# Attention scores and outputs in 64x32 tiles of TensorE, with f16 score operands and outputs in two banks by key half

## The reference

```
q, k, v = x_norm @ wq + bq, ctx @ wk + bk, ctx @ wv + bv      # 16 heads of 16
score = einsum('bhqd,bhkd->bhqk', q, k) / sqrt(16) + mask
out   = einsum('bhqk,bhkd->bhqd', softmax(score), v)
x = x + (out @ wo + bo)                                       # layer 0, layer 1 alike
x = x + shared_experts(xn) + top2_of_8_routed_experts(xn)     # layer 0
x = x + sqrt((xn @ cos(theta + tn))**2 + (xn @ sin(phi + pn))**2)   # layer 1
```

## Time and profile before

| | us |
|---|---|
| median of 3 runs | 1350.27 (1349.95 to 1350.47) |
| profiled execution | 1350.14, its span 1348.3 |
| TensorE busy | 1285.6 (95%), 9750 matmul records |
| ScalarE busy | 1036.6 (77%) |
| VectorE busy | 737.6 (55%) |
| exponentials L829 | 770.4, x832, 1.069 each |
| outputs L1560 | 448.6, x3328, 0.611 each |
| scores L1546 | 338.3, x1664, 0.470 each, idle before them 19.0 |

### The profile page before, as it was taken

One profiled execution on the slowest core, in us unless ns is written; L12 is line 12 of the kernel. 1 busy time (PEld: TensorE's weight loads), 2 busy tenths in 40 slices (PEclk: granted clock), 3 DMA queues, 4 the chain that ended last, 5 costly groups with the idle time before them and its releaser, 6 DMA issues. The chain is left out here.

```text
span 1348.3 us, 27233 instructions
## 1 busy us (share of the span) xinstructions
PE 1285.6 (95%) x9750; PEld 611.0 (45%) x9750; DVE 737.6 (55%) x1622; ACT 1036.6 (77%) x1482; POOL 178.4 (13%) x220
## 2 busy tenths in 40 slices
PE   8999999999999999998999999879989999999995
PEld 5422332332333466767999998522223323323322
DVE  5246577577466676446666666633424644443346
ACT  3689999999999754452666666348899999999993
POOL 4111120020020111331000010523300000000000
PEclk9999999999999999999999999868989999999997
DMA  7566744534537060313343452652210110010001
GB/s 222 131 209 219 232 127 152 181 95 155 178 103 265 32 204 17 110 48 102 98 128 114 116 146 79 140 154 70 82 33 1 44 40 1 32 51 1 1 1 62
DMA packets 105889, 140.78 MB, mean 104 GB/s; under 512 B 24916, under 2 KB 77523, under 8 KB 105791
## 3 DMA queue, kind: packets, MB, share of 16 engines
q1 hardware_dynamic: 88368, 102.13, 24.9%
q0 software_dynamic: 9888, 29.76, 7.0%
q10 hardware_dynamic: 7534, 7.57, 2.0%
HBM read 77.11 MB, written 51.69 MB: 96 GB/s over the span
## 5 line engine op out<-in xcount | busy, mean ns | idle before, releaser
L829 ACT ACTIVATE prob<-banks 128x1024 f32<-128x1024 f32 (+1 forms) x832 | 770.4, 1069 | 55.6 <-PE banks L1546 37.8
L1560 PE MATMUL banks<-prob,v 128*32 128x512 f32 (+1 forms) x3328 | 448.6, 611 | 1.1 <-ACT prob L829 1.1
L1546 PE MATMUL banks<-zone,kst 52*128 52x512 f32 (+1 forms) x1664 | 338.3, 470 | 19.0 <-ACT prob L829 17.3
L1546 PEld LDWEIGHTS banks<-zone,kst 52*128 52x128 f32 (+1 forms) x1664 | 138.6, 182 | 363.0 <-ACT prob L829 324.8
L2160 PE MATMUL banks<-xsT_d,w 128*128 128x128 f16 x1776 | 124.7, 220 | 3.2 <-issue 2.9
L1560 PEld LDWEIGHTS banks<-prob,v 128*32 128x32 f32 (+1 forms) x3328 | 65.7, 108 | 130.9 <-issue 108.0
L2160 PEld LDWEIGHTS banks<-xsT_d,w 128*128 128x128 f16 x1776 | 109.6, 98 | 12.6 <-issue 8.9
L2171 PE MATMUL banks<-w,hh 128*128 128x256 f16 x592 | 107.5, 274 | 0.0
L1070 DVE RECIPROCAL late<-late 128x512 f32<-128x512 f32 x31 | 103.9, 3353 | 1.1
L1967 DVE TENSOR_TENSOR hl<-hid,hh 128x128 f16<-128x128 f32 x296 | 83.3, 291 | 32.6 <-ACT hh L1898 24.9
L1065 DVE COPY late<-banks 128x512 f32<-128x512 f32 x31 | 21.4, 690 | 143.9 <-PE banks L1560 124.5
(11 more groups left out here) (270 smaller groups left out, 1281.1 us busy)
## 6 DMA issues: line engine op xcount, KB each, us to landing
weight_parts<-late SPq DMA_DIRECT2D x54, 256.0 KB, 3.3
w<-weight_parts POOLq DMA_DIRECT2D x24, 512.0 KB, 3.8
zone<-q_parts SPq DMA_DIRECT2D x180, 64.0 KB
late<-in_L_ffn_W_r SPq DMA_DIRECT2D x43, 256.0 KB, 4.0
kst<-kparts SPq DMA_DIRECT2D x88, 100.1 KB
q_parts<-qparts SPq DMA_DIRECT2D x16, 512.0 KB, 3.8
weight_parts<-more SPq DMA_DIRECT2D x26, 256.0 KB, 3.2
slot_rows<-late POOLq DMA_DIRECT2D x14, 384.0 KB, 4.2
```

Of the source, the lines that this page charges most:

```text
L829: nc.scalar.activation(prob[0:m, t % P_RING, 2 * (n % 2):2 * (n % 2) + 2, :], score[G % S_RING][0:m, :, :], ACT.Exp, scale=0.25 / WSCALE). ...
L1546: last = nc.tensor.matmul(score[G % S_RING][0:m, a, :], kst[stack, 2 * q + n % 2, t * P:t * P + m].bitcast(F32R), qst[stack, u % Q_RING, n ...
L1560: last = nc.tensor.matmul(outp[u % 2][GROUP * j:GROUP * (j + 1), :], v[0:m, t, u % NQ, j, :], prob[0:m, (u * KT + t) % P_RING, j, :], star ...
```

## The change

**Scores.** The operands in `kst`, `qst` and their DRAM copies are f16. A group is eight matmuls (L1570): 64x32 tiles, four slices of 32 keys by two heads, all with 512 queries. **Outputs** (L1585): eight 64x32 tiles, four heads by two halves of 64 keys; each half of the keys has its own bank, so an output takes two banks. `finish` copies the first (L1082) and adds the second (L1084). The last tile's unused rows of v and its ones are filled. **PSUM**: `S_RING` = 2 groups (four banks) and two outputs of two banks. **Order**: for each t now scores 2t+2, outputs t-1, scores 2t+3, then at most one side piece. **Side pieces** are spread (`SIDE_AT`, `OUT_AT`), the out-projection is cut into four calls instead of two for each i, and a piece waits for all pieces but the one before it. The scale of queries and the mask value fit f16; one more maximum enters the safety test ahead of the loop.

```diff
-S_RING = 3
+S_RING = 2
+BANKS = 8
-WAVE_AT = (2, 3, 5, 6, 8, 9)
+SIDE_AT = (2, 4, 6, 8, 9, 11)
+OUT_AT = (6, 8, 9, 11)
...
-                nc.vector.tensor_copy(osum, outp[u % 2]).then_inc(out_read, 1)
+                nc.vector.tensor_copy(osum, outp[u % 2][:, 0, :]).then_inc(half_read, 1)
+                dve.wait_ge(half_read, u + 1)
+                nc.vector.tensor_tensor(osum, osum, outp[u % 2][:, 1, :], ALU.add).then_inc(out_read, 1)
...
-                for a in range(2):
-                    stack = slice(HALF * a, HALF * a + STACK)
-                    last = nc.tensor.matmul(score[G % S_RING][0:m, a, :], kst[stack, 2 * q + n % 2, t * P:t * P + m].bitcast(F32R),
-                                            qst[stack, u % Q_RING, n % 2, :].bitcast(F32R), start=True, stop=True,
-                                            tile_position=(HALF * a, 0))
+                for j in range(0, m, GROUP):
+                    wide = min(GROUP, m - j)
+                    for a in range(2):
+                        stack = slice(HALF * a, HALF * a + STACK)
+                        last = nc.tensor.matmul(score[G % S_RING][j:j + wide, a, :], kst[stack, 2 * q + n % 2, t * P + j:t * P + j + wide],
+                                                qst[stack, u % Q_RING, n % 2, :], start=True, stop=True,
+                                                tile_position=(HALF * a, j))
...
-                for j in range(QH):
-                    last = nc.tensor.matmul(outp[u % 2][GROUP * j:GROUP * (j + 1), :], v[0:m, t, u % NQ, j, :],
-                                            prob[0:m, (u * KT + t) % P_RING, j, :], start=(t == 0), stop=(t == KT - 1),
-                                            tile_position=(0, GROUP * j))
+                for a in range(2):
+                    rows = slice(HALF * a, HALF * (a + 1))
+                    for j in range(QH):
+                        last = nc.tensor.matmul(outp[u % 2][GROUP * j:GROUP * (j + 1), a, :], v[rows, t, u % NQ, j, :],
+                                                prob[rows, (u * KT + t) % P_RING, j, :], start=(t == 0), stop=(t == KT - 1),
+                                                tile_position=(HALF * a, GROUP * j))
...
-                    if n:
-                        pe.wait_ge(side_free, n)
+                    if n >= 2:
+                        pe.wait_ge(side_free, n - 1)
...
+                if first:
+                    pieces = (outs[0:4], outs[4:8] + turns, asked[0:2] + back, asked[2:4] + logit)[q]
+                    times = (OUT_AT, SIDE_AT if done else SIDE_AT[1:], SIDE_AT, SIDE_AT)[q]
+                else:
+                    late = [] if done else turns
+                    pieces = ((turns if done else []) + outs[0:4], outs[4:8] + late + asked[0:2], asked[2:4] + back + waves[0:2], waves[2:8])[q]
+                    times = SIDE_AT
...
                 for t in range(KT):
-                    for G in (2 * (u * KT + t) + S_RING, 2 * (u * KT + t) + S_RING + 1):
-                        if G < UNITS * PAIRS:
-                            scores(G)
-                    outputs(u, t)
+                    G = 2 * (u * KT + t) + S_RING
+                    if G < UNITS * PAIRS:
+                        scores(G)
+                    if u or t:
+                        outputs((u * KT + t - 1) // KT, (t - 1) % KT)
+                    if G + 1 < UNITS * PAIRS:
+                        scores(G + 1)
+                    if t in pieces:
+                        side(*pieces[t])
+            outputs(UNITS - 1, KT - 1)
```

More of the change, by code:

```diff
@@ L51 @@
 WSCALE = 64.0
+QSCALE = 4.0
+FAR = 65504.0
+MASKED = 4e9 / FAR
 SAFE_SCORE = 68.0
@@ L209, in attention @@
         score = [banks[:, 2 * i:2 * i + 2, :] for i in range(S_RING)]
-        outp = [banks[:, 2 * S_RING + i, :] for i in range(2)]
+        outp = [banks[:, 2 * S_RING + 2 * i:2 * S_RING + 2 * i + 2, :] for i in range(2)]
+        project = [banks[:, BANKS - 2 + i, :] for i in range(2)]
         turn = [score[0][:, 0, :], score[0][:, 1, :]]
-        pj = [score[1][:, 0, :], score[1][:, 1, :], score[2][:, 0, :]]
-        nrm = score[2][:, 1, :]
+        pj = [banks[:, 2 + i, :] for i in range(3)]
+        nrm = banks[:, 5, :]
         slow_score = [banks[:, 4 * i:4 * i + 4, :].rearrange("p b s -> p (b s)") for i in range(2)]
@@ L592, in clear_values @@
                     nc.gpsimd.memset(beside(b), 1.0).then_inc(v_cleared, 1)
+                pool.wait_ge(v_cleared, 2)
+                nc.gpsimd.memset(v[HALF:P, KT - 1], 0.0).then_inc(v_cleared, 1)
+                for b in range(2):
+                    pool.wait_ge(v_cleared, 3 + b)
+                    nc.gpsimd.memset(beside(b)[HALF:KLAST, KT - 1:KT], 1.0).then_inc(v_cleared, 1)
+                pool.wait_ge(v_cleared, 5)
             def load_projection():
@@ L942, in _ @@
                     nc.vector.memset(beside(b), 1.0).then_inc(v_cleared, 1)
+                dve.wait_ge(v_cleared, 2)
+                nc.vector.memset(v[HALF:P, KT - 1], 0.0).then_inc(v_cleared, 1)
+                dve.wait_ge(v_cleared, 3)
+                for b in range(2):
+                    nc.vector.memset(beside(b)[HALF:KLAST, KT - 1:KT], 1.0).then_inc(v_cleared, 1)
             if first:
@@ L1476, in project_values @@
                 for h in range(DH):
-                    last = nc.tensor.matmul(outp[t % 2][0:m, 0:D], g.ctxT[:, h, t * P:t * P + m], wv[:, h, :],
+                    last = nc.tensor.matmul(project[t % 2][0:m, 0:D], g.ctxT[:, h, t * P:t * P + m], wv[:, h, :],
                                             start=(h == 0), stop=(h == DH - 1))
@@ L1585, in project_out @@
                 tokens = slice((2 * i + n) * P, (2 * i + n + 1) * P)
-                for k in range(DH):
-                    last = nc.tensor.matmul(bank[:, n * D:(n + 1) * D], packed(c, k)[:, tokens], wo[:, k, :], start=(k == 0), stop=(k == DH - 1))
-                if n:
+                last = nc.tensor.matmul(bank[:, n * D:(n + 1) * D], packed(c, k)[:, tokens], wo[:, k, :], start=(k == 0), stop=(k == DH - 1))
+                if n and k == DH - 1:
                     last.then_inc(side_done, 1)
@@ L1626, in _, with plan, side @@
             pe.wait_ge(shifts_loaded, 16 * 2 * NQ)
+            def plan(c, q):
+                ahead, done = c + 1 < NC, c >= 1
+                turns = [("turn", c + 1, 0), ("turn", c + 1, 1)] if ahead else []
+                outs = [("out", c - 1, i, n, k) for i in range(DH) for n in range(2) for k in range(DH)] if done else []
+                asked = [("query", c + 1, o, k) for o in range(DH) for k in range(DH)] if ahead else []
+                back = [("xturn", c - 1, 0), ("xturn", c - 1, 1)] if done else []
+                waves = [("wave", c - 1, i, h) for i in range(TPC) for h in range(DH)] if done and not first else []
+                logit = [("logit", c - 1)] if done and first else []
+                if first:
[5 more added lines that the diff above has]
+                    times = SIDE_AT
+                return {t: piece for t, piece in zip(times, pieces)}
+            def side(name, c, *at_piece):
+                if name == "turn":
+                    if at_piece[0] == 0:
+                        pe.wait_ge(xn_ready, TPC * (c + 1))
+                    turn_tokens(name, c, at_piece[0], xn)
+                if name == "out":
+                    project_out(c, *at_piece)
+                if name == "query":
+                    query(c, *at_piece)
+                if name == "xturn":
+                    if at_piece[0] == 0:
+                        pe.wait_ge(on_ready, TPC * (c + 1))
+                    turn_tokens(name, c, at_piece[0], on)
+                if name == "logit":
+                    logits(c)
+                if name == "wave":
+                    wave(c, *at_piece)
             for G in range(S_RING):
@@ L1700, in _ @@
                 for n in range(2):
-                    project_out(c, i, n)
+                    for k in range(DH):
+                        project_out(c, i, n, k)
             hidden_ahead(6, 12)
```

153 lines of the change are left out of this document (64 added, 89 removed).

## The result

The changed kernel takes 1383.02 us (median of four runs, 1381.04 to 1384.16) against 1350.11 before: ratio 1.0245, interval 1.0228 to 1.0263, slower. Its span is 1379.1, 30.8 more. The forecast was 1360, 10 us more than before, with a range of its own of 1352 to 1372. The kernel is slower, as forecast, but by 33 us: outside that range, and inside the wide one of 1326 to 1396 only.

What follows compares the result with a forecast made beforehand. ScalarE's exponentials, one per 0.906 us, were taken to set the pace. The terms +15 - 33 - 3.6 + 23 + 8 + 1 = +10.4 on 1350.14 gave 1360 us; own range 1352 to 1372, wide range 1326 to 1396.

Steps and rivals of the forecast that it cites:

- Step 4: Layer 0: a unit's first side piece waits for VectorE's read of its bank, +23 us (0 to 30); layer 1 nothing.
- rival E: Layer 1's three waits for another queue grow as more instructions are wanted: 5 to 15 us more; chance 0.13 with C.
- step 2: Two score slots instead of three: the chain takes 2.79 us where ScalarE wants 2.72, +15 us (0 to +36).
- hold of unit 1: Layer 0: a piece no longer waits for the piece just before it, so this hold goes, -3.6 us.
- half clock behind: The clock falls behind each hold by VectorE; five more holds cost +8 us (0 to 12).
- 5 and the experts: Ends: tail output read twice more, a maximum and memsets before the loop, +1 us (0 to 3); experts had no term.
- Step 1: TensorE's stream of a step where it is behind: 1.31 us (1.28 to 1.66) instead of 1.66, in one tiling.
- Step 3: Both loops: spread side pieces cost 14.4 us instead of 47, -33; sign: ScalarE's idle for scores a third of before.
- Rival A: Faster: VectorE isn't late and the ring closes in 2.72 us or little more; 1328 us, chance 0.28.
- C: Much slower: a pass's 64x32 tiles start one by one, 21 us more and some 4 at the sides; 1385, chance 0.13.
- D: Each matmul takes 0.062 us, so a step's 32 need 1.97 against 1.81: 67 us, 1412; chance 0.04.

Runs made afterwards that it cites:

- Runs 1, 2 and 9: Changed kernel with all old side-piece places: 1343.53 us; changed kernel with layer 0's first pieces late: 1347.49; kernel of f16 operands alone with the change's places: 1356.15.

## Why the prediction was wrong

Step 4 failed. Side pieces that wait for VectorE were priced at 23 us in layer 0 and at nothing in layer 1, and cost 36 and 7. The 8 us beside the gathers (rival E) were left out of the sum, and side work saved 5 us less than forecast. Against them stands step 2, whose 15 us did not come at all. Without that false term the same sum would have been 10.4 - 15 = -4.6, faster than before: that the forecast pointed the right way is luck.

By its own steps, in us; the measured column sums what the distances between exponentials have over 0.906.

| step | forecast | measured |
|---|---|---|
| 2, ring of two | +15 | 0 |
| 3, side work | -33 | -28 |
| 3, hold of unit 1 | -3.6 | -4 |
| 4, VectorE, layer 0 | +23 | +36 |
| 4, VectorE, layer 1 | 0 | +7 |
| 4, half clock behind | +8 | +10 |
| 5 and the experts | +1 | +2 |
| rival E, beside the gathers | 0 | +8 |
| sum | +10 | +31 |

- **Step 1** held (1.32 put together, against 1.31) but is hardly ever reached. Its sign was about 1.3 from output to output where TensorE is behind: one step between tiles of 128 keys took 1.29, from 1099.60 to 1100.89, where ScalarE had freed both slots during a hold. All others at full clock took 1.55 or more, no less than the 1.53 of f16 alone with wide tiles: the room that the small tiles make is used up by the ring of two.
- **Step 2 failed in its sum.** The chain was right piece by piece and too long as a whole. In the stretch above it is 1.18 (exponential to score), 0.23, 0.86 and 0.47 (score to exponential), 2.74 and not 2.79; elsewhere the first piece takes as little as 1.07. All tiles start together, where I had added 0.05. At 2.72 it hides, and what is left of the 15 us is under 1. A margin of 0.07 on a sum of latencies was no ground for 15 us, and the wide tiles show how near the edge it is: 0.09 and 0.16 more in the chain cost 17 to 34 us.
- **Step 3** held roughly: of side work's 47 us some 19 are left, where 14.4 were forecast. A half of the out-projection or a turn costs 0 to 0.23, a query or wave part 0.1 to 0.35. Its sign, a third of before in units 4 to 15 of layer 1, came out at 10.1 of 26.4 us, without the two holds there.
- **Step 4 had the right mechanism, and priced it too small.** Runs 1, 2 and 9 settle it from three sides: undo all places, undo the waiting ones alone, put the places alone into another kernel. Unit 5 came out as worked (6.61 for 6.6), in part by luck: its piece reached VectorE 0.6 us before the unit began, not 1.1, and from there to the read took 11.95, not 12.6. Unit 6 was 5.37 and not 4.1: VectorE took the turn at 204.48, when the unit began, not 1.1 before. It had waited 9.74 us for unit 5's last out piece, took it at 198.32 and was busy from there to the turn without a gap (a normalisation, two cuts, the first turn), 6.16 us. I had put the turn at the time when TensorE is done with it, not when VectorE gets to it. Unit 14 (5.8 us of ScalarE) I had left out, as it has no turns before it, though unit 13's out pieces and their cuts are queued there; likewise layer 1's unit 12 (4.3), whose out pieces move from t=6 to t=2 when there are no turns ahead of them (TensorE stands 3.54 us there, for the divided output of chunk 2 and not for a bank), and unit 6 (2.7), whose first output waits for a query part queued behind the gathers' sums on VectorE. And ScalarE loses 0.5 to 1.1 us more than TensorE stands: the out piece behind the hold took 1.22 us and not the 0.70 of its like at full clock.
- **Rival E came in**: 92.5 to 100.6 beside the gathers; where no kernel was held there, the change cost 2.0% instead of 2.45%.
- **Rival A** is what the same kernel does with the places undone: 1343.5, not 1328; E's 8 us and the pairs of pieces are most of the difference. **C and D** fell: tiles of a pass start together, and a step leaves TensorE 0.34 us idle. Its 32 records are 24 instructions, since each fp32 output shows two, which I had counted as matmuls; at D's own 0.062 they need 1.49 us, under 1.81, so by its own price D would have cost nothing. The Trainium skill ("TensorE: Matmul & The Clock Gate", part 1) gives about 62 ns a matmul where matmuls are decoded in software, which as an estimate would spread the eight tiles of a score group over 0.5 us; they start within 0.03.

What none of the steps said: f16 operands alone give 1.5 to 1.7%, more than any variant with small tiles and a ring of two gave (0.8% at best).

## What to carry to other kernels

When side work moves in an in-order queue, follow the queue that consumes it to its next point of release, and ask when that queue gets to a piece, not only when the piece is done; do it for every list that changes, the short cases of first and last chunk too. Of a change made of several parts, price each alone: here the operands' type gave 1.5 to 1.7%, the small tiles shortened a chain that the ring of two made longer, and a list of times took 3%. Run a chain of latencies with a margin under its own error as two cases, not as a term.

## What the runs showed of the hardware

- Eight 64x32 tiles on two halves of the rows and four column groups start within 0.03 us and write two banks together; a group of 512 columns takes 0.41 us from first start to last end, as one 64x128 pair does (0.39).
- Changing between 64x32 and 64x128, and between 64x32 and 128x32, costs about 0.1 us from score to output and 0.13 to 0.16 from output to score.
- Behind TensorE's stand of 6.61 us the granted clock was 0.50 (1.2 GHz) for the next 4 us, and ScalarE lost some 2 us there beyond the hold; the first output group of layer 0's loop, after a start with score groups alone, took 1.93 us as well.
- Units 0 to 2 of layer 1 need 70.7 us at ScalarE's pace. The changed kernel took 100.6 in one execution and 76.9 in another, f16 alone 86.0 and 76.0 on one chip; in the changed kernel's long one TensorE's weight loads came with 0.6 to 1.3 us of idle time before each and nothing seen to wait for.
